# Interaction kernel on one core: right fields of chunks 4 and 5 loaded by DMA instead of picked by TensorE, their products placed later, and the last product in halves that TensorE sums

## The reference

```python
X0 = inputs.reshape(-1, NUM_FIELDS, EMBED_DIM)
Xi = X0
pools = []
for W, b in ((W1, b1), (W2, b2), (W3, b3)):
    out_ch = W.shape[0]
    m = Xi.shape[1]
    Wr = W.reshape(out_ch, NUM_FIELDS, m)
    Xi = jnp.einsum('bhd,bmd,ohm->bod', X0, Xi, Wr) + b[None, :, None]
    pools.append(Xi.sum(axis=-1))
concat = jnp.concatenate(pools, axis=-1)
return concat @ fc_W.T + fc_b
```

## Time and profile before

| | us |
| --- | --- |
| median of 3 runs (83.08 to 83.12) | 83.09 |
| the profiled execution | 83.07 |
| its span | 81.3 |

### The profile page before, as it was taken

The page is one execution under the profiler, slowest core; times in us unless marked ns, Lnnn a source line. Parts: engine busy times, 40 slices in busy tenths (PEclk is TensorE's granted clock), DMA queues, the critical chain, the costliest instruction groups (busy, mean ns, idle before and its releaser), DMA issues.

```text
span 81.3 us, 1119 instructions
## 1 busy us (share of the span) xinstructions
PE 75.0 (92%) x367; PEld 52.0 (64%) x367; DVE 47.4 (58%) x44; ACT 34.6 (43%) x51; POOL 49.6 (61%) x49
## 2 busy tenths in 40 slices
PE   4999999699999999979999999999999999999911
PEld 1335456654327767658888888888888888877600
DVE  1056998499979999597499519962002003303581
ACT  1830983968798945973756300470300300000000
POOL 4986497999992599590099889449906006064200
PEclk9999999999999999999999999999999999999999
DMA  0898999999986525259993000000000000000000
GB/s 23 283 338 249 371 366 353 383 388 387 378 261 201 157 61 141 84 149 411 370 384 153 0 4 0 4 0 0 0 0 0 0 8 0 0 0 0 0 0 0
DMA packets 7530, 12.01 MB, mean 148 GB/s; under 512 B 836, under 2 KB 3972, under 8 KB 7268
## 3 DMA queue, kind: packets, MB, share of 16 engines
q1 hardware_dynamic: 6915, 11.16, 40.0%
q10 hardware_dynamic: 608, 0.77, 3.1%
HBM read 10.88 MB, written 1.05 MB: 147 GB/s over the span
## 4 chain that ended last, share of the span: by engine, by line
PE 75%; ACT 8%; DMA 7%; DVE 4%; issue 2%; ACTq 2%; SPq 1%; DVEq 0%
PE a_ps L576 27%; PE x_ps L576 24%; DMA w_sb<-w 7%; PE z_ps L570 7%; PE a_ps L661 5%; ACT feat L357 4%; PE a_ps L634 3%; PE x_ps L596 2%; PE a_ps L623 2%; PE a_ps L622 2%; ACTq L429 2%; DVE w_sb L511 1%; DVE total L549 1%; ACT zz L357 1%; DVE x L501 1%
## 5 line engine op out<-in xcount | busy, mean ns | idle before, releaser
L265 POOL TENSOR_TENSOR feat<-r_in,feat 128x1024 fp32r<-128x1024 f32 x8 | 19.2, 2403 | 3.8 <-ACT feat L357 3.2
L576 PE MATMUL x_ps<-feat,w_hi 128*128 128x512 f32 x64 | 18.9, 395 | 0.2 <-ACT feat L357 0.2
L501 DVE SCALAR_TENSOR_TENSOR x<-a_ps,vec,x 128x512 f32<-128x512 f32 x8 | 6.0, 751 | 19.8 <-PE a_ps L623 19.7
L258 POOL TENSOR_TENSOR xs<-x_in,xs 32x512 fp32r<-32x512 f32 x7 | 11.1, 1585 | 8.8 <-ACT xs L357 8.4
L576 PE MATMUL a_ps<-feat,a_hi 128*128 128x512 f32 x64 | 16.2, 396 | 0.0
L272 POOL TENSOR_TENSOR x<-x 128x512 f32<-128x512 f32 x6 | 7.8, 1292 | 11.5 <-DVE x L501 11.3
L576 PEld LDWEIGHTS x_ps<-feat,w_hi 128*128 128x128 f32 x64 | 11.9, 188 | 3.2 <-issue 0.6
L576 PEld LDWEIGHTS a_ps<-feat,a_hi 128*128 128x128 f32 x64 | 11.9, 188 | 2.7
L481 DVE TENSOR_TENSOR feat<-z_ps,feat 128x1024 fp32r<-128x1024 f32 x8 | 9.8, 1219 | 2.2 <-ACT feat L357 2.2
L357 ACT ACTIVATE feat<-z_ps 128x1024 fp32r<-128x1024 f32 x8 | 8.2, 1021 | 6.0 <-DVE z_ps L474 5.1
L371 ACT ACTIVATE x<-x_ps,vec 128x512 f32<-128x512 f32 x8 | 5.4, 685 | 12.3 <-PE x_ps L596 12.3
(11 more groups left out here) (74 smaller groups left out, 75.7 us busy)
## 6 DMA issues: line engine op xcount, KB each, us to landing
w_sb<-w SPq DMA_DIRECT2D x9, 512.0 KB, 8.5
x_in<-xl SPq DMA_DIRECT2D x8, 256.0 KB, 7.2
r_in<-xr SPq DMA_DIRECT2D x2, 1024.0 KB, 6.2
a_by_fields<-at_sb SPq DMA_DIRECT2D x8, 96.0 KB, 2.0
x<-x ACTq DMA_DIRECT2D x1, 512.0 KB, 4.6
x<-x SPq DMA_DIRECT2D x1, 512.0 KB, 5.7
w_sb<-w SPq DMA_DIRECT2D x1, 256.0 KB, 11.1
a_by_fields<-at_sb SPq DMA_DIRECT2D x4, 64.0 KB, 1.9
```

The costliest lines, as they stand in the source:

```text
L258: nc.gpsimd.tensor_tensor(xs[rows, c, :], x_in[rows, c % X_BUFS, :], xs[rows, c, :].bitcast(f32), ALU.subtract).then_inc(xs_lo, 1)
L265: nc.gpsimd.tensor_tensor(feat[:, c, 1, of_half(1), :], z_of(c, 1), feat[:, c, 0, of_half(1), :].bitcast(f32), ALU.subtract).then_inc(lo_d ...
L501: nc.vector.scalar_tensor_tensor(out=x1[:, c, :], in0=a_ps[:, c % 2, :], scalar=vec[:, 3:4], in1=x1[:, c, :], op0=ALU.add, op1=ALU.mult).t ...
L576: nc.tensor.matmul(bank, weights[:, k, :], feat[:, c, part, k, :], start=(start and k == 0), stop=False)
```

## The change

`PICKED` falls from 6 to 4. TensorE no longer does `pick_right` for chunks 4 and 5 (8 matmuls). `load_right` now also loads chunks 4 and 5, 1 MB each: that of chunk 4 behind the rest of W1 and ahead of `load_x(5)`, that of chunk 5 where that of chunk 6 was. Each further one waits until its buffer's former chunk is done, so `load_right(7)` waits for `hi(5, 1)` and for GpSimd's `lo(5)`. `mult(4, .)` and `mult(5, .)` take their right operand from SBUF (`r_in`) instead of PSUM. On VectorE `chunk(5)` moves behind the work on `f1`. On ScalarE `split_x(4)`, `hi(5, .)` and `split_x(5)` move behind the copy of `q`, and on GpSimd `split_x(4)` and `split_x(5)` move behind `lo(4)`. At the end `product(7)` is done in two halves of 256 columns, and 8 small matmuls with `ones` add its eight groups of 64 columns into `y_ps`, in place of VectorE's `tensor_reduce` and one matmul.

```diff
--- before.py
+++ after.py
@@ -25,7 +25,7 @@
 TERM_HI, TERM_LO, TERM_HI2, TERMS = 0, 32, 64, 96
 
 
-PICKED = 6
+PICKED = 4
 X_BUFS = 4
 
 
@@ -100,7 +100,7 @@
         q_sb = sb("q_sb", [P, 1])
         ones = sb("ones", [P, 1])
         xsum = sb("xsum", [P, B])
-        total = sb("total", [P, 2, B])
+        total = sb("total", [P, B])
         y_sb = sb("y_sb", [1, B])
         fcb_sb = sb("fcb_sb", [1, 1])
 
@@ -134,6 +134,7 @@
         q_ready, q_saved, a_ready, a_saved = sem("q_ready"), sem("q_saved"), sem("a_ready"), sem("a_saved")
         x1_ready, x1_saved = sem("x1_ready"), sem("x1_saved")
         b_ready, prod_done, acc_done = sem("b_ready"), sem("prod_done"), sem("acc_done")
+        last_done = sem("last_done")
         total_done, y_ready, y_done = sem("total_done"), sem("y_ready"), sem("y_done")
         ZEROS, A_OUT, F_MAIN, F_REST = 4, 16 * 12, 16 * 2 * J, 16 * 5
 
@@ -182,11 +183,12 @@
                 sp.dma_start(x_in[:, c % X_BUFS, :], xl[:, c * N:(c + 1) * N]).then_inc(x_here[c % X_BUFS], 16)
 
             def load_right(c):
-                if c % 2 == 0:
+
+                if c == PICKED:
                     sp.wait_ge(spread_done, 3)
                 else:
-                    sp.wait_ge(hi_done, count(PICKED - 1, 1))
-                    sp.wait_ge(lo_done[1], PICKED)
+                    sp.wait_ge(hi_done, count(max(c - 2, PICKED - 1), 1))
+                    sp.wait_ge(lo_done[1], max(c - 1, PICKED))
                 sp.dma_start(r_in[:, c % 2, :, :], xr[c]).then_inc(r_here[c % 2], 16)
 
             def load_w3(i):
@@ -219,6 +221,7 @@
             load_w2(2)
             load_w2(3)
             sp.dma_start(w1_sb[:, :, EVEN:, :], w1[:, :, EVEN:, :]).then_inc(w1_rest_in, 16)
+            load_right(4)
             load_x(5)
             load_x(6)
             for t in range(ROUNDS):
@@ -237,12 +240,13 @@
                         scratch.tensor, first * M, [[0, 3], [(EXT + 1) * M, HALF], [1, M]])).then_inc(f_rest_in, 16)
             sp.dma_start(f1[0:TERMS, LIN, :], bass.AP(
                 scratch.tensor, FC2_COL * EXT * M, [[0, 3], [M, H], [1, M]])).then_inc(f_rest_in, 16)
-            load_right(PICKED)
+            load_right(5)
             sp.wait_ge(lo16_done, 1)
             sp.dma_start(x16[:, :, :].rearrange("p g n -> p (g n)"),
                          x.rearrange("h (c n) -> (h c) n", c=4)).then_inc(xp_in, 16)
             load_x(7)
-            load_right(PICKED + 1)
+            load_right(6)
+            load_right(7)
             sp.dma_start(fcb_sb[:, :], fc_b).then_inc(fcb_in, 16)
             sp.wait_ge(y_done, 1)
             sp.dma_start(out, y_sb[:, :]).then_inc(out_done, 16)
@@ -317,17 +321,17 @@
             pool.wait_ge(xs_lo, 4)
             lo(1)
             pool.wait_ge(lo_done[1], 2)
-            split_x(4)
-            pool.wait_ge(xs_lo, 5)
             lo(2)
             pool.wait_ge(w1_rest_in, 16)
             nc.gpsimd.tensor_tensor(w1_sb[:, 0, EVEN:, :], w1_sb[:, 0, EVEN:, :], w1_sb[:, 1, EVEN:, :],
                                     ALU.add).then_inc(w_sum, 1)
             pool.wait_ge(w_sum, 2)
+            lo(3)
+            lo(4)
+            pool.wait_ge(lo_done[1], 5)
+            split_x(4)
             split_x(5)
             pool.wait_ge(xs_lo, 6)
-            lo(3)
-            lo(4)
             lo(5)
             pool.wait_ge(lo_done[1], 6)
             split_x(6)
@@ -416,7 +419,6 @@
             hi(3, 1)
             act.wait_ge(w_sum, 2)
             copy(w1_hi[:, EVEN:, :], w1_sb[:, 0, EVEN:, :]).then_inc(w_hi_done, 1)
-            split_x(5)
             hi(4, 0)
             hi(4, 1)
             act.wait_ge(vec_in, 16)
@@ -428,8 +430,6 @@
                 k = 1 if j == 0 else 0
                 act.dma_start(f2[H * j:H * j + H, k:TILES, :], bass.AP(
                     scratch.tensor, (TILES * j + k) * M, [[(EXT + 1) * M, H], [1, (TILES - k) * M]])).then_inc(f_main_in, 16)
-            hi(5, 0)
-            hi(5, 1)
             save_zz(1)
             act.wait_ge(v_saved, 1)
             copy(v_rep[:, :, :], v_st[:, 0:H].rearrange("o (h r) -> o h r", r=1).to_broadcast(
@@ -440,10 +440,14 @@
             save_x1(3)
             act.wait_ge(f_sum, 2)
             copy(a_hi[0:TERMS, TILES:, :], f1[0:TERMS, TILES:, :]).then_inc(a_hi_done, 1)
-            split_x(6)
             save_x1(4)
             act.wait_ge(q_ready, 1)
             copy(q_sb[:, :], q_ps).then_inc(q_saved, 1)
+            split_x(4)
+            hi(5, 0)
+            hi(5, 1)
+            split_x(5)
+            split_x(6)
             hi(6, 0)
             hi(6, 1)
             split_x(7)
@@ -465,7 +469,7 @@
                         dve.wait_ge(hi_done, count(c - 2, 1))
                         dve.wait_ge(lo_done[1], c - 1)
                 else:
-                    dve.wait_ge(r_here[c % 2], 16)
+                    dve.wait_ge(r_here[c % 2], 16 * ((c - PICKED) // 2 + 1))
                     right = r_in[:, c % 2, tiles, :]
                     if half == 0:
                         dve.wait_ge(z_done, count(c - 1, 1))
@@ -523,7 +527,6 @@
             dve.wait_ge(w_hi_done, 2)
             rest_lo(w1_sb[:, 0, :, :], w1_hi, w_lo_done)
             lo(4)
-            chunk(5)
             dve.wait_ge(f_main_in, F_MAIN)
             nc.vector.tensor_tensor(f1[:, 0:TILES, :], f1[:, 0:TILES, :], f2[:, 0:TILES, :], ALU.add).then_inc(f_sum, 1)
             dve.wait_ge(f_rest_in, F_REST)
@@ -535,6 +538,7 @@
             dve.wait_ge(f_sum, 2)
             dve.wait_ge(a_hi_done, 2)
             rest_lo(f1, a_hi, a_lo_done)
+            chunk(5)
             chunk(6)
             product(0)
             product(1)
@@ -542,12 +546,15 @@
             for c in range(2, CHUNKS - 1):
                 product(c)
             dve.wait_ge(acc_done, CHUNKS - 2)
-            nc.vector.tensor_reduce(total[:, 0, :], x1[:, 0, :].rearrange("p (d b) -> p b d", b=B),
+            nc.vector.tensor_reduce(total[:, :], x1[:, 0, :].rearrange("p (d b) -> p b d", b=B),
                                     axis=AX.X, op=ALU.add).then_inc(total_done, 1)
-            product(CHUNKS - 1)
-            dve.wait_ge(prod_done, CHUNKS)
-            nc.vector.tensor_reduce(total[:, 1, :], x1[:, CHUNKS - 1, :].rearrange("p (d b) -> p b d", b=B),
-                                    axis=AX.X, op=ALU.add).then_inc(total_done, 1)
+            dve.wait_ge(x1_saved, CHUNKS)
+            dve.wait_ge(b_ready, CHUNKS)
+            for half in range(HALVES):
+                cols = slice(half * N // 2, (half + 1) * N // 2)
+                nc.vector.scalar_tensor_tensor(out=x1[:, CHUNKS - 1, cols], in0=a_ps[:, (CHUNKS - 1) % 2, cols],
+                                               scalar=vec[:, 3:4], in1=x1[:, CHUNKS - 1, cols], op0=ALU.add,
+                                               op1=ALU.mult).then_inc(last_done, 1)
             dve.wait_ge(y_ready, 1)
             dve.wait_ge(fcb_in, 16)
             nc.vector.tensor_scalar(y_sb[:, :], y_ps, fcb_sb[:, 0:1], 0.0, ALU.add, ALU.add).then_inc(y_done, 1)
@@ -689,17 +696,13 @@
             pick_right(3, 1)
             a_round(2)
             a_round(3)
-            pick_right(4, 0)
             x1_lo(0, 1)
-            pick_right(4, 1)
             x1_hi(1, 0)
             x1_lo(1, 0)
             x1_hi(1, 1)
-            pick_right(5, 0)
             x1_lo(1, 1)
             x1_tail(0)
             x1_tail(1)
-            pick_right(5, 1)
             spread16(1)
             x1_product(2)
             x1_product(3)
@@ -726,9 +729,13 @@
             nc.tensor.matmul(y_ps, q_sb[:, :], xsum[:, :], start=False, stop=False)
             a_product(CHUNKS - 1)
             pe.wait_ge(ones_done, 1)
-            for i in range(2):
-                pe.wait_ge(total_done, i + 1)
-                last = nc.tensor.matmul(y_ps, ones[:, :], total[:, i, :], start=False, stop=(i == 1))
+            pe.wait_ge(total_done, 1)
+            nc.tensor.matmul(y_ps, ones[:, :], total[:, :], start=False, stop=False)
+            for d in range(N // B):
+                if d % (N // B // HALVES) == 0:
+                    pe.wait_ge(last_done, d // (N // B // HALVES) + 1)
+                last = nc.tensor.matmul(y_ps, ones[:, :], x1[:, CHUNKS - 1, d * B:(d + 1) * B],
+                                        start=False, stop=(d == N // B - 1))
             last.then_inc(y_ready, 1)
 
 
```

## The result

The changed kernel takes 87.49 us (median of 4 runs: 86.77, 86.97, 88.01, 88.02), the kernel before 83.09. The ratio is 1.052, interval 1.043 to 1.062. It is 4.4 us slower, where 1.9 us slower was forecast. The executions lie in two pairs, 86.8 to 87.0 and 88.0.

The account below looks back on a forecast made before the run. TensorE was taken to bound the kernel from 40 to 77.3 us, then the chain behind `a_product(7)`. 83.07 + 2.4 (TensorE late) - 0.5 (shorter end) = 85.0 us; range 83.3 to 86.0.

Parts of the forecast that it names:

- the block in front: Ahead of `x1_tail(0)`: `mult(4, .)` and GpSimd's `lo(3)` alternate, `rest_lo` ends at 31.3, TensorE waits from 27.9.
- The clock falls: Rival, chance 0.09: behind the pause 13 matmuls run at 1.2 GHz, 3.0 us more; 88.0 us.
- The main case: Whole kernel at 85.0 us, chance 0.52, own range 84.3 to 85.8; TensorE stands still from 28.1 to 31.3.
- the term at `x1_product(3)`: Front stage: `x1_product(3)` starts at 35.8 instead of 35.49, costing 0.3 us in all.
- the chain of chunks 5 to 7: Behind the copy of `q`, GpSimd and VectorE alternate; late `lo(5)`, `lo(6)`, `lo(7)` leave TensorE 2.4 us late in all.
- The third loss: At `x1_lo(7, 1)`: `lo(7)` ends at 65.2, so TensorE gets there at 65.25 instead of 62.84.
- From `a_product(4)` on TensorE has all its inputs: Behind chunk 7's stall: no further wait, and TensorE keeps its offset of 2.4 us.
- the end: Behind `a_product(7)`: halved product and small matmuls make the end shorter by 0.5 us.
- The prediction's bounds for it: Gain at the end between 0.1 us (halves of 0.65) and 0.7.
- the `zz` wait of 0.57 us: At `x1_tail(2)`: TensorE's wait for ScalarE's copy of `zz`, 0.57 us before, is gone.

Follow-up runs that it names:

- The kernel with `lo(3)` waiting: The changed kernel, but at the front GpSimd starts `lo(3)` only when `rest_lo` is done; 87.37 us.
- Filling the pause: The changed kernel with 12 matmuls into an unused PSUM bank ahead of `x1_tail(0)`; 86.27 us, ratio 1.039.
- GpSimd's new order: The changed kernel, GpSimd doing sums of x behind `lo(4)`, then `lo(5)`, `lo(6)`, the four `split_x`, `lo(7)`; ScalarE's `save_x1(5)` ahead of `hi(7, 0)`; 85.73 us.
- Second half freed alone: The changed kernel with GpSimd's splits last, chunk 6 loaded directly behind chunk 5, `product(0)` ahead of `chunk(6)`, `save_x1(5)` early; 84.40 us, ratio 1.016.
- Front freed then: The changed kernel with those four second-half edits, and `lo(3)` waiting for `rest_lo`; 82.13 us, ratio 0.989.
- the last order: The changed kernel with freed second half and `lo(3)` behind `rest_lo`, GpSimd's sums of x between `lo(5)` and `lo(6)`; 80.94 us, ratio 0.974.

## Why the prediction was wrong

**Right: the block in front.** Chunk 4 landed at 25.9 (26.4 expected), the two engines alternated, and `rest_lo` ended at 30.96, in the range of 30.9 to 31.6. TensorE stood still for 3.0 us. The kernel with `lo(3)` waiting shows the cause: the same operands, no block, 1.22 us instead of 3.39. The Trainium skill's rule for two SBUF inputs (SBUF — State Buffer, "Who interferes with whom") is what the runs showed.

**Wrong: the clock, the first failed step.** "The clock falls" was a rival with a chance of 0.09. The main case had a pause of over 3 us, yet a full clock behind it, and so put the price of a fall at nothing. In the profile the clock fell and cost 1.41 us in `x1_product(2)` and 0.2 in the spread matmuls ahead of it, less than the 3.0 priced, because it rose again after some eight matmuls. Filling the pause kept it up in three of four executions. The Trainium skill's warning (TensorE: Matmul & The Clock Gate, "Why this matters for your kernels") held: the clock fell behind the pause of 3.0 to 3.5 us, or in its last 0.1 us, in each of the four profiles of a kernel that kept it open. It also fell behind a wait of 2.76 us, and behind waits of 1.34 and 1.91 us shortly after one another; it fell behind none of 1.5 us or less that stood alone. I had taken "no row shows a fall" as evidence, when no row showed such a pause either. With the fall the term at `x1_product(3)` was +1.67, not +0.3: 1.6 for the clock, less some 0.2 because `rest_lo` was done at 30.96 and not at 31.3.

**Wrong in one link: the chain of chunks 5 to 7.** Its mechanism was right. It begins behind the copy of `q`, which waits for `x1_product(4)`, so it moved with the late front (`q` was copied at 43.89, 42.55 expected) and its losses came on top. `lo(5)` came 0.57 us late for TensorE (0.4 expected) and `lo(6)` 0.94 (0.9). The third loss was 1.04 instead of 0.8, with another last link: `x1_product(7)` needs `save_x1(5)`, which stands behind `hi(7, 1)` on ScalarE; the prediction asked only for `lo(7)`. This was shown by moving it: the wait of 0.81 us went, and one of 0.44 us for `lo(7)` took its place. My step "From `a_product(4)` on TensorE has all its inputs" was right.

**Right: the end**, 0.52 us (0.5), and 0.48 alone. The prediction's bounds for it don't follow from its own rows: two halves at the whole 0.76 us each would make the end 0.1 us longer, not 0.1 shorter. Both halves took 0.88 us together. The bounds named for its main case also add up to 86.1 at the top, not 85.8.

The sum of the profiled run is 1.67 + 0.57 + 0.94 + 1.04 - 0.52 = 3.70, against 0.3 + 0.4 + 0.9 + 0.8 - 0.5 = 1.9. The main case was off by 1.4 at the front, which is the clock, and by 0.4 in the chain.

**The two runs of 88.0 us** have a mean clock of 0.96, the other two 0.98. A mean of 0.98 over 85 us is an estimated 3.4 us at half speed, which is what the profile shows; 0.96 would be twice that. So in these two the clock was probably down for twice as long. Where is not settled, since neither was profiled. The mean alone doesn't price it: executions of the kernel before had mean clocks from 0.987 to 1.00 and times within 0.2 us of each other, and with GpSimd's new order 85.08 and 87.18 us came with 0.976 and 0.980. So these kernels spread for another reason too, which stays open.

**What each loss is worth depends on the other.** Front freed alone: 0.1 us at the median, 0.8 in the best execution. Second half freed alone: 3.1 us (87.49 to 84.40). Front freed then: 2.3, and 3.5 with the last order as well (80.94). The picks' 1.8 us (8 matmuls at 0.23) and the `zz` wait of 0.57 were a real gain; in the changed kernel more than they gave was lost by the start of `x1_product(3)`.

**Left open.** When the clock falls behind a pause was not measured beyond these cases. Nor was it shown why one of four executions with the filled pause still had a mean clock of 0.98.

## What to carry to other kernels

Before a vector operand is moved from PSUM to SBUF, list what GpSimd does at that moment, and who waits for the vector operation behind it: here 1.2 us became 3.4 and a TensorE pause of 3 us. When a change makes the bounding engine wait for several microseconds at once, add the price of a slower clock behind the wait, even if the profile has never shown one. And when removing one loss brings nothing, look for the second that covered it; order the helpers by when their results are wanted.

## What the runs showed of the hardware

Six profiles show the clock at half while TensorE has work, each once, for 3.4 us. Against the moment at which TensorE worked again it halved 1.3 us later in the changed kernel, 1.4 and 0.6 later in two others with pauses of 3.5 and 3.3 us, 0.6 later behind the wait of 2.76 us, and 0.1 and 0.2 us before it with GpSimd's new order (`lo(3)` in its old and its new place). So a fall need not come in the pause itself, and its moment varies between kernels with nearly the same pause.

VectorE's multiplications with both operands in SBUF and GpSimd's operations took turns when both had one waiting: 1.24, 3.00, 3.39 us, where undisturbed ones take 1.2 (`mult`) and 2.4 (`lo`).

The megabyte for chunk 4 took between 12.7 and 13.2 us from issue to landing in eleven profiles of the same load at the same place, and the first tail moved by as much (31.10 to 31.63 us in the profiles with the open pause).
